# The experts' silu of the first mixture: one silu call between two table loads, or exp, ln and exp in the table set that stands, with a product more on VectorE

## The reference, cut to what matters

```
h = _rmsnorm(x, ln2_w).reshape(-1, HID)
...
for e in range(E):
    w1 = w13[e, :FFN]
    w3 = w13[e, FFN:]
    g = jax.nn.silu(h @ w1.T) * (h @ w3.T)
    out = out + jnp.einsum('tf,hf->th', g, w2[e]) * wfull[:, e:e + 1]
return x + out.reshape(B, S, HID)
```

## Time and profile before

| | |
|---|---|
| median of 3 runs | 2976.07 us (2974.56 to 2987.31) |
| profiled execution | 2984.2 us, its span 2982.4 us |
| PE matmul busy | 2628.4 us (88%) |
| DVE busy | 1508.0 us (51%) |
| ACT busy | 1546.9 us (52%) |
| POOL busy | 77.0 us (3%) |
| DMA, mean | 29 GB/s |
| mean granted TensorE clock | 0.923 |

### The profile page before, as it was taken

How to read it: one execution, slowest core, us unless ns; L and a number is a source line. 1 busy time by engine, 2 the same in 40 slices (tenths; PEclk the granted TensorE clock), 3 DMA queues, 4 the chain that set the end, 5 groups by cost and what they waited for, 6 DMA issues and landing times.

```text
span 2982.4 us, 54432 instructions
## 1 busy us (share of the span) xinstructions
PE 2628.4 (88%) x21104; PEld 1976.2 (66%) x21120; DVE 1508.0 (51%) x3781; ACT 1546.9 (52%) x2721; POOL 77.0 (3%) x40
## 2 busy tenths in 40 slices
PE   4789898989989898998989999898999989899586
PEld 3447667666766766676676767767676775767455
DVE  4345555464555546556554645544455644545140
ACT  1526474563737456373745637374463746537242
POOL 0000000000000000000000000000000000000000
PEclk9779999898999999999998999999999999999787
DMA  3000100101010010101001010100101000010101
GB/s 143 10 7 1 36 26 30 32 9 38 17 37 26 23 40 9 36 19 37 26 23 39 9 36 19 37 25 16 47 2 39 23 30 33 9 52 2 50 9 45
DMA packets 31411, 85.37 MB, mean 29 GB/s; under 512 B 4127, under 2 KB 13351, under 8 KB 30632
## 3 DMA queue, kind: packets, MB, share of 16 engines
q1 hardware_dynamic: 31144, 81.64, 8.2%
HBM read 79.53 MB, written 2.10 MB: 27 GB/s over the span
## 4 chain that ended last, share of the span: by engine, by line
PE 69%; DVE 10%; ACT 8%; issue 7%; DMA 5%; SPq 1%; DVEq 0%; ACTq 0%
PE psum L486 9%; PE psum L493 7%; DMA ew<-in_ew 5%; PE psum L688 4%; PE psum L548 4%; PE psum L466 3%; PE psum L648 3%; PE psum L518 3%; PE psum L792 2%; PE psum L635 2%; PE psum L536 2%; PE psum L473 2%; PE psum L619 2%; PE psum L739 2%; PE psum L556 2%
## 5 line engine op out<-in xcount | busy, mean ns | idle before, releaser
L892 ACT ACTIVATE gbuf<-psum,cols 128x256 f32<-128x256 f32 x512 | 202.7, 475 | 697.8 <-PE psum L493 680.1
L486 PE MATMUL psum<-x1T_s,ew 128*128 128x256 f32 x1024 | 301.5, 449 | 84.0 <-DMA ew<-in_ew 58.2
L486 PEld LDWEIGHTS psum<-x1T_s,ew 128*128 128x128 f32 x1024 | 217.3, 222 | 163.9 <-DMA ew<-in_ew 66.8
L1154 DVE SCALAR_TENSOR_TENSOR acc<-psum,small,acc 128x128 f32<-128x128 f32 x256 | 78.0, 346 | 431.2 <-PE psum L493 431.2
L493 PEld LDWEIGHTS psum<-ew,gbuf 128*128 128x128 f32 x2048 | 266.7, 204 | 14.1 <-ACT gbuf L892 5.3
L493 PE MATMUL psum<-ew,gbuf 128*128 128x128 f32 x2048 | 265.6, 286 | 4.1 <-ACT gbuf L892 4.1
L466 PE MATMUL psum<-hT_s,w13T 128*128 128x256 f32 x1024 | 242.7, 383 | 0.0
L466 PEld LDWEIGHTS psum<-hT_s,w13T 128*128 128x128 f32 x1024 | 191.0, 192 | 43.6 <-issue 22.1
L878 ACT ACT_TABLE_LOAD x144 | 184.8, 1283 | 2.6
L874 ACT ACT_TABLE_LOAD x128 | 164.2, 1283 | 2.2 <-PE psum L466 0.6
L1129 DVE TENSOR_TENSOR gbuf<-gbuf,psum 128x512 f32<-128x512 f32 x128 | 87.8, 686 | 145.2 <-ACT gbuf L874 145.2
(11 more groups left out here) (212 smaller groups left out, 4742.7 us busy)
## 6 DMA issues: line engine op xcount, KB each, us to landing
ew<-in_ew SPq DMA_DIRECT2D x128, 512.0 KB, 3.5
x<-in_x SPq DMA_DIRECT2D x16, 128.0 KB, 2.1
w13T<-in_w13T SPq DMA_DIRECT2D x1, 2048.0 KB
lqkvg<-in_lqkvg SPq DMA_DIRECT2D x1, 2048.0 KB
out<-y SPq DMA_DIRECT2D x16, 128.0 KB, 1.8
wqkv<-in_wqkv SPq DMA_DIRECT2D x1, 1536.0 KB, 6.5
w2T<-in_w2T SPq DMA_DIRECT2D x1, 1024.0 KB
wrope<-in_wrope SPq DMA_DIRECT2D x1, 640.0 KB, 7.5
```

The costliest lines, as they stand in the source:

```text
L486: last = mm(bank(f"h{e}{j}")[:, a * N:(a + 1) * N], ew[:, e % 2, c * P:(c + 1) * P], x1T[:, :], start=True, stop=True)
L892: ins = af(r1[:, c, :], bank(f"h{e}{j}")[:, a * N:(a + 1) * N], ACT.Relu, bias=cols[:, 8 + 4 * e + c:9 + 4 * e + c])
```

## The change

For each expert, ACT no longer calls silu. It writes exp(-a) into `g0`, then ln(1 + that), then exp of minus that, which is 1 / (1 + exp(-a)), each waiting for the one before. DVE multiplies the result by a, read from bank a(e), which it now frees in place of ACT, and then by b(e) as before. The preload of the exp and ln set after each expert is dropped and stays only behind the silu of the sum in `moe0(8)`. Two counters of semaphores (`act_chain`, `gate_ready`) are booked for stage B.

```diff
-    "B": {"dve_chain": 10, "sg_ready": 1},
+    "B": {"act_chain": 16, "dve_chain": 10, "gate_ready": 8, "sg_ready": 1},
...
                         act.wait_ge(*filled(f"y{e - 2}"))
-                    af(g0[:, e % 2, :, :], bank(f"a{e}").rearrange("p (c n) -> p c n", c=2), ACT.Silu).then_inc(*frees(f"a{e}"))
+                    gs = g0[:, e % 2, :, :]
+                    af(gs, bank(f"a{e}").rearrange("p (c n) -> p c n", c=2), ACT.Exp, scale=-1.0).then_inc(*signals("act_chain"))
+                    act.wait_ge(*chained("act_chain"))
+                    af(gs, gs, ACT.Ln, bias=1.0).then_inc(*signals("act_chain"))
+                    act.wait_ge(*chained("act_chain"))
+                    af(gs, gs, ACT.Exp, scale=-1.0).then_inc(*signals("gate_ready"))
                 else:
                     act.wait_ge(*read_out(f"y{E - 1}"))
                     af(sg[:, :, :], acc0[:, :, :], ACT.Silu).then_inc(*signals("sg_ready"))
-                act.preload_act_table_set("natural_log_exp_and_others")
+                    act.preload_act_table_set("natural_log_exp_and_others")
...
                     dve.wait_ge(*filled(f"b{e}"))
+                    dve.wait_ge(*given("gate_ready", e + 1))
+                    gs = g0[:, e % 2, :, :]
+                    v.tensor_tensor(gs, gs, bank(f"a{e}").rearrange("p (c n) -> p c n", c=2), ALU.mult).then_inc(*frees(f"a{e}"))
                     dve.wait_ge(*read_out(f"a{e}"))
-                    gs = g0[:, e % 2, :, :]
                     v.tensor_tensor(gs, gs, bank(f"b{e}").rearrange("p (c n) -> p c n", c=2), ALU.mult).then_inc(*frees(f"b{e}"))
```

## The result

The changed kernel takes 3009.54 us (3005.74 to 3012.21, 5 runs) against 2982.41 us (2974.56 to 2987.31, 5 runs) of the kernel before on the same chip: ratio 1.0091, 95% interval 1.0065 to 1.0117. It is slower by 0.9%, and the forecast of 3003 (+0.9%) holds. The profiled execution has a span of 3004.0 us against 2982.4.

What follows compares the result with a forecast made beforehand. PE, 69% of the chain, was taken to bound the kernel, with ACT half idle. 0.54 + 0.50 + 0.72 = 1.76 a body, x 15 = 26.4, less 2.7 = +24, plus 3 for clock: 3003 us against the median, range 2983 to 3023.

Steps and rivals of the forecast that it cites:

- the gate, from a(e) seen: ScalarE's exp, ln, exp per expert: 2.02 us from a(e) being visible to the gate, which comes no sooner than before.
- ScalarE's relief, whole kernel: Dropping two loads and a silu for three calls relieves ACT of 1.15 us per expert, 128 times, 147 us.
- experts 0 and 1: Woven body: y(0) starts 1.09 us late, y(1) gives part back by no longer waiting; +0.54 us, ends +0.3 and +1.1.
- expert 3, te00: te00 waits for bank a(3), now freed by DVE's new product behind its backlog: +0.42 to +0.62, taken +0.50 us.
- experts 4 to 6: DVE ends 0.72 later at each, covered by PE's longer products: taken 0, up to 0.3 us a body at expert 5.
- expert 7: The new product delays DVE's L1441, for which f0 waits on PE: +0.72 us, ends 0.65 and 0.85.
- AB, once: In AB ACT alone sets the pace of 3.20 us per expert; now PE needs 2.72: -2.7 us, ends -4 and 0.
- clock: Longer idle time ahead of f0 makes more bodies slow: 0.2 us a body, +3 in all, ends 0 and +25.
- Only one place counts: Rival: late y(0) is made up and te00 is not late, leaving 15 x 0.72 - 2.7 = +8, 2984 us; chance 0.13.
- ScalarE's backlog: Rival: ACT's backlog paces the start of C, so its relief makes the kernel faster, 2933 us, or 2955 if half; chance 0.05.
- The loads stay: Rival: table loads remain between or around Ln and Exp, at least 15 x 2.6 = 38 us more, 3040; chance 0.02.
- Clock: Rival: longer idle time in front of f0 turns nearly all bodies slow, 25 us in place of 3, 3025; chance 0.10.

Runs made afterwards that it cites:

- ScalarE's part alone: Changed kernel with VectorE's product with a left out, exp, ln, exp and the dropped loads kept: 2967.96 us, ratio to before 0.9929.
- the filling: Kernel before plus unused TensorE products into the eighth bank, three ahead of the wait for z2_ready, one ahead of z2T: 2961.45 us, ratio 0.9953.
- three places mended: Changed kernel with a copied on VectorE for experts 0 and 1, on ScalarE for expert 3, z2T scaled ahead of expert 7: 2969.45 us, ratio 0.9980.
- four mended and filled: Changed kernel with copies for experts 0, 1, 5, expert 3's work reordered, z2T scaled earlier, three unused TensorE products ahead of z2_ready: 2962.76 us, ratio 0.9949.
- z2T moved and filled: Kernel before with z2T scaled ahead of expert 7 and three unused TensorE products ahead of the wait for z2_ready: 2961.03 us, ratio 0.9943.
- the product alone: Kernel before with silu and both table loads kept and only VectorE's product with a added: 3013.6 us, ratio 1.0084.

## Why the prediction was right

Point by point, in the order of its steps, per body where not said otherwise:

| step | predicted | measured |
|---|---|---|
| the gate, from a(e) seen | 2.02 | 1.92 (1105.82 to 1107.74 in expert 0) |
| ScalarE's relief, whole kernel | 147, gaps between calls counted | 169 of busy time |
| product, dependent | 0.72 | 0.72 (1174.93 to 1175.65) |
| experts 0 and 1 | +0.54 | +0.35 |
| expert 3, te00 | +0.50 | +0.42 |
| te01 and te10, behind te00 | 0 | +0.11 |
| experts 4 to 6 | 0, up to 0.3 | +0.21 |
| expert 7 | +0.72 | +0.62 |
| sum of a woven body | +1.76 | +1.71 |
| AB, once | -2.7 | -2.4 at the last y |
| clock | +0.2 | not separable (time at 1.2 GHz +0.3; body +1.82, places +1.71) |

The places and the mechanism are right: DVE is late by one product, and PE waits for it at y(0), te00 and f0. That the sum came so close is partly luck. Its three terms were 0.37 us too high together, and two that it put at nothing came to 0.32. And a body does not follow its waits this closely: it holds the pause at the top of the loop, which no term has, and the kernel with 0.74 us less and without that pause took the same 177.5.

The largest error in the prices is that of Ln: 632 + 93 = 725 ns for one with a bias, and 630 measured. The 93 came from L857, whose bias is a column of a tile; 1.0 is not one. This makes y(0) earlier by 0.1, and L857 and f0 with it by 0.1. The other 0.1 at the first place is y(1) itself: no longer started out of a wait, it takes 1.05 us and not 1.16. That y(1) would wait no more, and so give back its 0.38, came as worked out.

What was taken as covered and was not is DVE's lateness behind expert 3 and at expert 5; "from here to the state products PE runs without a wait for DVE" was wrong. The bank ring was followed only to te00; te01 and te10 wait as well, 0.11. The kernel without the product for these two experts shows that both terms are theirs. At expert 5 the bound of 0.3 held. Part of the 0.72 is made up there because the state product no longer meets GpSimd's work. Before and after, on DVE:

```profile
1148.35 1.34 DVE L1409 TENSOR_TENSOR st<-st,cd 128x512 f32<-128x512 f32 x1
```

```profile
1155.65 0.69 DVE L1416 TENSOR_TENSOR st<-st,cd 128x512 f32<-128x512 f32 x1
```

GpSimd's two products ran until 1149.14 before and until 1155.52 after.

The rivals. *Only one place counts* fell: y(0) and te00 are late. *ScalarE's backlog* fell as a reason for a faster kernel, but not entirely: with ScalarE's part alone the kernel is faster by 0.7%, of which its places account for half: y(1)'s wait of 0.38, 0.11 at expert 7 and AB, and not the 1.15 per expert of relief. *The loads stay* fell. *Clock* did not come in the form in which it was put: time at 1.2 GHz grew by 0.3 us a body only. But it is what decides how much of a change of 1 us a body arrives. The two kinds of bodies of the earlier trace rows are the ends of a range in the kernel before, 172.1 to 177.7; in the changed kernel all 13 took 177.2 to 178.1, and the body of 175.8 that was foretold for the fast kind never came.

Two lengths recur in the records. One is 176.8 to 178.1 us: all 13 bodies of the changed kernel, and of the one without the product for experts 3 and 5 in both its profiles. The other is 173.7 to 174.6 us: all 13 bodies of the kernel before with the filling, and 11, 11 and 12 of the 13 with three places mended, with four mended and filled, and with z2T moved and filled. In the changed kernel the long stretch at 1.2 GHz begins 147.8 to 148.4 us behind the z products in every body, in the kernel before anywhere from 142.0 to 148.6. So the bodies of some kernels settle at a length, with the changes of level at a fixed distance from the idle places; that the one holds the other there was only argued, and no experiment separates it.

## What to carry to other kernels

Count what an operation costs on each engine, and then ask at each place who waits for that engine next: 169 us of ScalarE were bought for 78 us of VectorE, and it was mostly the latter that stood in front of TensorE (+1.9 us a body for the product alone, -0.5 for ScalarE's part alone). When the reader that frees a PSUM bank changes, the next uses of that bank and of its neighbours wait for the new reader's queue, not for its operation. Where TensorE's clock changes level inside a loop body, compare fixed stretches at one level first and the whole time second: here a gain of 0.74 us in 177 did not show at all. And look at the waits that no term of the sum is about: a pause of some 0.9 us came and went from one kernel to the next.

## What the runs showed of the hardware

An Ln with bias 1.0 costs the same 630 ns as an Exp with none, where a bias read from a column adds 93 ns (298 against 205). A table load takes 1283 ns and nothing beside it: silus with two loads each follow every 3.20 us. A VectorE product of two SBUF tensors took 1.34 us beside GpSimd's work, and 0.69 without it. Keeping TensorE busy with products that nobody reads made the kernel before 0.5% faster, and the changed kernel not. VectorE paused for 0.8 to 1.1 us at one place of the loop with nothing awaited that the profile shows, in four of the kernels here and in no other.
